# Leaving out TensorE waits that another wait of the same chunk already implies, in a retention layer with a mixture of experts

## The chip, the cores and the metric

The kernel runs on one core of one Trainium2 chip. The metric is the device time of one execution in microseconds (us), the median of several runs. Before the change it is 790.35 us (three runs, 789.27 to 793.92).

## The reference, cut to what matters

The input x has 4 sequences of 1024 tokens with 256 features, all fp32. It is normalised, and two branches read the result: a retention block (attention with a fixed decay instead of a softmax) and a mixture of eight experts with two chosen for each token. The output is x plus both branches.

```
xn = layernorm(x)
# retention: 16 heads of 16
q, k, v = xn @ W_q.T, xn @ W_k.T, xn @ W_v.T
attn = (q @ k.T) * gamma[h] ** (i - j) for j <= i, else 0, divided by sqrt(16)
y = attn @ v, normalised by sequence and head, times gn_weight, plus gn_bias
a = y @ W_o.T
# experts
probs = softmax(xn @ gate_w.T + gate_b); the two largest are kept
f = sum over the two of prob * (relu(xn @ w1[e] + b1[e]) @ w2[e] + b2[e])
out = x + a + f
```

## The kernel before, in words

The kernel is written engine by engine: each engine has its own program, in an order written out by hand, and all coupling goes through semaphores. An engine's `wait_ge(s, n)` holds back all that stands behind it in that engine's program. There is no planner.

The work has four stages. First comes the layer norm and the routing of the tokens to experts. Then comes retention, in 32 chunks of 128 tokens: chunks 0 to 3 and 28 to 31 are written out, chunks 4 to 27 are a loop whose body holds two chunks (`run_steps(pe, 0, NT, 4, 28, chunk)`, line 855). Then come 39 slots of 256 token rows through the experts' two layers (lines 744 and 648), and last the output projection (line 908).

Retention keeps, for each pair of heads, a running state, so that a chunk needs only its own scores and the state. TensorE's order in chunk i is: query projection of chunk i+1 (line 717), key transposes of i+1 (754), the part of the output that comes from the state (`across`, 784), transposes of the tokens of i+2 (695), query transposes of i+1 (760), the new state's sums (807), the part of the output from inside the chunk (`inside`, 796), the scores of i+1 (`scores`, 773), key and value projection of i+2 (704). The results in PSUM are taken out by ScalarE (ACT) and VectorE (DVE): ACT copies the transposed queries into a masked layout in two instructions (`diagonal_queries`, line 539), which the scores of the same chunk need; DVE masks the scores (1084), makes keys and queries from the projections (1072, 1078), and keeps the state (1090, 1096).

GpSimd (POOL) works beside it: for each chunk it issues two indirect DMAs (line 427) that scatter the chunk's normalised rows to their experts' slots. SyncE starts the loads for that scatter when TensorE has signalled the token transposes (`xt_psum`), so the scatter runs at the chunks' pace, about one chunk behind.

The scores are sixteen matmuls in the trace (eight in the source; an fp32 matmul appears as two): four groups of 32 rows of the array, one for each group of four heads, two column blocks each.
Of the kernel before, what the change touches and what calls it, by code (L numbers as in the profile page):

```python
# [36 lines left out]
NT = B * T // P  # L37
# [4 lines left out]
NB = H // HB  # L42
QH = 2
# [68 lines left out]
def wait(eng, sem, value):  # L112

    if isinstance(value, int) and value <= 0:
        return
    eng.wait_ge(sem, value)

def build(nc, where, x, wq_t, wkv_t, wo_t, gn, gate_t, gate_b, w1, w2, b1, b2, const, out):
# [9 lines left out]
    with ExitStack() as ctx:  # L129
# [30 lines left out]
        y_t = xn[:].rearrange("p t (c i) -> p t c i", c=KC)  # L160
# [45 lines left out]
        s_f = ff(NB, HB * P)  # L206
# [4 lines left out]
        q_diag = ff(2, KC, QH * P)  # L211
# [4 lines left out]
        def v_own(par, c=None):  # L216
            pairs = H // QH if c is None else HP // QH
            return bass.AP(v_pad.tensor, v_pad[:, par, (c or 0) * HP * 2 * DH:(c or 0) * HP * 2 * DH + 1].offset,
                           [list(v_pad.ap[0]), [QH * 2 * DH, pairs], [3 * DH, QH], [1, DH]])
# [40 lines left out]
        s = {}  # L260
# [380 lines left out]
        def _(pe):  # L641
# [55 lines left out]

            def key_value_projection(n, par):

                pe.wait_ge(s["xt_h"], n + 1)  # L700
                pe.wait_ge(s["xt_l"], n + 1)
                for m, (a, b) in enumerate(PASSES):
                    for k in range(KC):
                        last = pe.matmul(ps[:, 4, :], xt[:, par, a, k * P:(k + 1) * P], wkv[:, b, k, :],  # L704
                                         start=(m == 0 and k == 0), stop=(m == 2 and k == KC - 1))
                last.then_inc(s["kv_psum"], 1)

            def query_projection(n, par):

                pe.wait_ge(s["xt_h"], n + 1)  # L710
                pe.wait_ge(s["xt_l"], n + 1)

                wait(pe, s["q_t"], n)
                wait(pe, s["q_diag"], QH * n)
                for m, (a, b) in enumerate(PASSES):
                    for k in range(KC):
                        last = pe.matmul(ps[:, 5, 0:D], xt[:, par, a, k * P:(k + 1) * P], wq[:, b, k, :],  # L717
                                         start=(m == 0 and k == 0), stop=(m == 2 and k == KC - 1))
                last.then_inc(s["q_psum"], 1)
# [28 lines left out]

            def key_transposes(n, par):
                pe.wait_ge(s["k_f"], n + 1)  # L750

                wait(pe, s["st_t"], n - 1)
                for c in range(KC):
                    last = pe.transpose(ps[:, 6, c * P:(c + 1) * P], kq_f[:, par, c * P:(c + 1) * P], ident)  # L754
                last.then_inc(s["kt_psum"], 1)
# [6 lines left out]

            def scores(n, par):

                pe.wait_ge(s["k_t"], n + 1)
                pe.wait_ge(s["q_diag"], QH * (n + 1))
                for c in range(KC):
                    for g in range(NB):
                        rows = slice(g * QR, (g + 1) * QR)
                        if c == 0:  # L770

                            wait(pe, s["s_f"], NB * (n - 1) + g + 1 if not isinstance(n, int) or n > 0 else 0)
                        last = pe.matmul(ps[:, g, c * QH * P:(c + 1) * QH * P], kq_t[rows, par, 0, c * P:(c + 1) * P],  # L773
                                         q_diag[rows, par, c], start=True, stop=True)
                        if c == KC - 1:
                            last.then_inc(s["s_psum"], 1)

            def across(n, par):
                pe.wait_ge(s["st_f"], n + 1)
                pe.wait_ge(s["q_t"], n + 1)  # L780

                wait(pe, s["y_t"], n)
                for c in range(KC):
                    last = pe.matmul(ps[:, 7, c * P:(c + 1) * P], state_f[:, c], kq_t[:, par, 1, c * P:(c + 1) * P],  # L784
                                     start=(c == 0), stop=False, skip_group_check=True)
                last.then_inc(s["across_done"], 1)

            def inside(n, par):
                pe.wait_ge(s["s_f"], NB * (n + 1))
                pe.wait_ge(s["v"], n + 1)  # L790

                for c in range(KC):
                    for o in range(QH):
                        for g in range(NB):
                            h = c * HP + g * QH + o
                            last = pe.matmul(ps[g * QR:(g + 1) * QR, 7, c * P:(c + 1) * P], v_pad[:, par, h * 2 * DH:(h + 1) * 2 * DH],  # L796
                                             s_f[:, g, (c * QH + o) * P:(c * QH + o + 1) * P], start=False,
                                             stop=(c == KC - 1 and o == QH - 1), skip_group_check=True)
                last.then_inc(s["y_psum"], 1)

            def state_sums(n, par):
                pe.wait_ge(s["k_f"], n + 1)
                pe.wait_ge(s["v"], n + 1)

                pe.wait_ge(s["k_t"], min(n + 2, NT) if isinstance(n, int) else n + 2)
                for c in range(KC):
                    last = pe.matmul(ps[:, 6, 256 + c * P:256 + (c + 1) * P], kq_f[:, par, c * P:(c + 1) * P], v_own(par, c),  # L807
                                     start=(c == 0), stop=(c == KC - 1), skip_group_check=True)
                last.then_inc(s["u_psum"], 1)

            def chunk(i, par):
                if within(i + 1, NT):
                    query_projection(i + 1, 1 - par)
                if within(i + 1, NT):
                    key_transposes(i + 1, 1 - par)
                if within(i, NT):
                    across(i, par)
                if within(i + 2, NT):
                    x_transposes(i + 2, par)
                if within(i + 1, NT):  # L820
                    query_transposes(i + 1, 1 - par)
                if within(i, NT - 1):
                    state_sums(i, par)
                if isinstance(i, int) and i == NT - 1:
                    layer1(0, 0, (0, 1))
                if within(i, NT):
                    inside(i, par)
                if within(i + 1, NT):
                    scores(i + 1, 1 - par)
                if isinstance(i, int) and i == NT - 2:  # L830
                    pe.wait_ge(s["v"], NT)
                    slot_transposes(0, 0)
                if within(i + 2, NT):
                    key_value_projection(i + 2, par)
# [4 lines left out]
            pe.wait_ge(s["w_split_h"], 3)  # L839
            pe.wait_ge(s["w_split_l"], 3)  # L840
            key_value_projection(0, 0)
            query_projection(0, 0)

            pe.wait_ge(s["route_mask"], 1)
            pe.wait_ge(s["tables_done"], 3)
            for k in range(2):
                last = pe.matmul(ps[:, 1 + k, 0:NT * E], token_sets[:, k], mask_bf[:], start=True, stop=True)
            last.then_inc(s["route_psum"], 1)
            key_transposes(0, 0)
            x_transposes(1, 1)  # L850
            query_transposes(0, 0)
            pe.wait_ge(s["rows_done"], 2)
            scores(0, 0)
            key_value_projection(1, 1)
            run_steps(pe, 0, NT, 4, 28, chunk)

# [442 lines left out]
```

## Time and profile before

| | |
|---|---|
| median of 3 runs | 790.35 us |
| profiled execution, its own time | 788.52 us |
| its span, first to last instruction | 786.7 us |
| mean granted TensorE clock | 0.974 |
| TensorE matmul busy | 732.9 us (93%) |
| VectorE busy | 584.2 us (74%) |
| ScalarE busy | 498.2 us (63%) |
| GpSimd busy | 283.1 us (36%) |

The median is over other executions than the profiled one, which took 788.52 us. A busy time counts the engine's own instructions; waits, register instructions and DMA issues are not in it. The end of a matmul in the trace is modelled, so a signal that a matmul gives is best read from the instruction that waited for it. In the timeline, neighbouring instructions of one line are merged into one row.

### The profile page before, as it was taken

How to read it: one execution, taken by the hardware profiler on the slowest of the kernel's cores; microseconds unless marked ns; L12 is line 12 of the kernel's file. 1: busy time of each engine (PE TensorE's matmuls, PEld its weight loads, DVE VectorE, ACT ScalarE, POOL GpSimd, SP SyncE). 2: the span in 40 equal slices, each digit the busy share in tenths (PEclk: the TensorE clock that was granted, in tenths of full speed). 3: DMA queues.
4: the chain of work that ended last, by engine and by line, in shares of the span. 5: the costliest groups of instructions: out<-in, count | busy, mean ns of one | idle time of the engine just before them, and what ended most of it. 6: DMA issues, size and time to landing. Idle time of an engine off the chain costs nothing.

```text
span 786.7 us, 20206 instructions
## 1 busy us (share of the span) xinstructions
PE 732.9 (93%) x6588; PEld 678.4 (86%) x6588; DVE 584.2 (74%) x1024; ACT 498.2 (63%) x880; POOL 283.1 (36%) x225
## 2 busy tenths in 40 slices
PE   2948999999999988999999999999999999999967
PEld 1426788888887788999999999999999999999957
DVE  6776777777777776877877878777778778778545
ACT  3832334333333386787787787887877877877780
POOL 0013333333334313344344354353353453443420
PEclk9977999999999998999999999999999999999988
DMA  9995333333334485788888888788888888886249
GB/s 294 371 335 176 119 105 108 98 103 101 101 101 136 157 299 150 227 218 252 213 232 251 206 236 257 184 250 242 208 247 239 213 249 227 217 252 173 35 109 332
DMA packets 89047, 157.85 MB, mean 201 GB/s; under 512 B 26496, under 2 KB 66560, under 8 KB 78976
## 3 DMA queue, kind: packets, MB, share of 16 engines
q1 hardware_dynamic: 74720, 138.87, 53.8%
q0 software_dynamic: 14304, 18.69, 14.5%
q8 instruction: 13, 0.21, 0.1%
q14 instruction: 10, 0.08, 0.0%
HBM read 111.67 MB, written 37.37 MB: 189 GB/s over the span
## 4 chain that ended last, share of the span: by engine, by line
PE 85%; DVE 5%; issue 4%; ACT 2%; DMA 2%; POOL 0%; SPq 0%; POOLq 0%; ACTq 0%; DVEq 0%; another core or an unknown queue 0%
PE ps L744 28%; PE ps L648 27%; PE ps L704 6%; PE ps L773 6%; PE ps L717 3%; PE ps L796 3%; PE ps L760 2%; PE ps L908 2%; PE ps L729 2%; PE ps L784 2%; PE ps L666 1%; PE ps L754 1%; PE ps L807 1%; ACT arena_f L539 1%; DMA xn<-x 1%
## 5 line engine op out<-in xcount | busy, mean ns | idle before, releaser
L648 PE MATMUL ps<-arena_r 128*128 128x256 f32 x1872 | 235.2, 286 | 2.2 <-DVE arena_r L1184 2.2
L744 PE MATMUL ps<-arena_r 128*128 128x256 f32 x1872 | 233.4, 285 | 1.9 <-DVE arena_r L1101 1.1
L744 PEld LDWEIGHTS ps<-arena_r 128*128 128x128 f32 x1872 | 229.5, 194 | 2.4 <-issue 2.4
L648 PEld LDWEIGHTS ps<-arena_r 128*128 128x128 f32 x1872 | 228.3, 193 | 2.4 <-issue 2.4
L444 POOL TENSOR_TENSOR fence_out<-eps_col 128x1 f32<-128x1 f32 x39 | 78.7, 2019 | 274.6 <-DVE arena_f L1160 274.6
L498 ACT ACTIVATE arena_r<-arena_f 128x2048 fp32r<-128x2048 f32 x77 | 143.7, 1921 | 0.0
L446 POOL DMA_INDIRECT sum_rows<-arena_f,pair_slot x78 | 122.7, 1574 | 18.1 <-issue 17.3
L580 ACT ACTIVATE arena_f<-ps,arena_f 128x256 f32<-128x256 f32 x156 | 65.3, 471 | 90.5 <-PE ps L744 79.5
L1176 DVE TENSOR_TENSOR arena_r<-arena_f,arena_r 128x2048 fp32r<-128x2048 f32 x39 | 89.4, 2292 | 38.7 <-ACT arena_r L498 38.7
L1184 DVE TENSOR_TENSOR arena_r<-arena_f,arena_r 128x512 fp32r<-128x512 f32 x78 | 55.9, 717 | 53.7 <-ACT arena_r L588 51.9
L1084 DVE TENSOR_TENSOR arena_f<-ps,cst 128x512 f32<-128x512 f32 x128 | 84.7, 683 | 14.9 <-PE ps L773 14.9
L1172 DVE TENSOR_TENSOR arena_r<-arena_f,arena_r 128x2048 fp32r<-128x2048 f32 x38 | 86.8, 2285 | 1.0 <-ACT arena_r L498 1.0
L520 ACT ACTIVATE arena_f<-ps 128x256 f32<-128x256 f32 x32 | 12.3, 384 | 95.0 <-DVE arena_f L1072 81.8
L427 POOL DMA_INDIRECT xs_rows<-pair_chunk,row_chunk x64 | 62.4, 976 | 20.7 <-issue 20.3
L580 ACT ACTIVATE pair_chunk<-ps,arena_f 128x256 f32<-128x256 f32 x156 | 65.5, 472 | 3.3
L1184 DVE TENSOR_TENSOR arena_r<-pair_chunk,arena_r 128x512 fp32r<-128x512 f32 x78 | 50.4, 688 | 12.8 <-ACT arena_r L588 12.8
L773 PE MATMUL ps<-arena_f 32*128 32x256 f32 x512 | 46.2, 409 | 14.4 <-DVE rows L1050 9.2
L704 PE MATMUL ps<-wkv,arena_r 128*128 128x512 f32 x192 | 54.4, 419 | 1.0 <-DVE arena_r L1065 1.0
L773 PEld LDWEIGHTS ps<-arena_f 32*128 32x128 f32 x512 | 30.8, 188 | 24.1 <-issue 13.7
L425 POOL TENSOR_TENSOR fence_out<-eps_col 128x1 f32<-128x1 f32 x32 | 6.1, 190 | 123.5 <-DMA row_chunk<-rows 123.0
L704 PEld LDWEIGHTS ps<-wkv,arena_r 128*128 128x128 f32 x192 | 34.3, 192 | 17.6 <-issue 11.8
L588 ACT ACTIVATE arena_r<-arena_f 128x512 fp32r<-128x512 f32 x78 | 49.3, 632 | 0.0
(134 smaller groups left out, 855.2 us busy)
## 6 DMA issues: line engine op xcount, KB each, us to landing
arena_f<-w SPq DMA_DIRECT2D x78, 1024.0 KB
xs_rows<-spare_rows SPq DMA_DIRECT2D x39, 258.0 KB, 3.6
arena_f<-xs_rows SPq DMA_DIRECT2D x39, 258.0 KB, 3.8
pair_chunk<-xn SPq DMA_DIRECT2D x32, 256.0 KB, 2.6
arena_f<-b SPq DMA_DIRECT2D x39, 128.0 KB, 4.0
xn<-x SPq DMA_DIRECT2D x8, 512.0 KB, 8.8
x_chunk<-xn SPq DMA_DIRECT2D x32, 128.0 KB
arena_f<-sum_rows SPq DMA_DIRECT2D x8, 512.0 KB, 7.6
```

Source lines behind the costliest of these rows:

```text
L444: nc.gpsimd.tensor_tensor(fence_out[:, 0:1], eps_col[:], eps_col[:], ALU.add).then_inc(s["fence"], 1)
L446: nc.gpsimd.indirect_dma_start(sum_rows, bass.IndirectOffsetOnAxis(ap=pair_slot[:, par, j:j + 1], axis=0), ys[:, j * D:(j + 1) * D], None, ...
L498: nc.scalar.activation(parts_[par][:, 0], raw[par], ACT.Copy).then_inc(s[f"w{k + 1}_h"], 1)
L580: last = nc.scalar.activation(h_f[hp][:, o * SLOT:(o + 1) * SLOT], ps[:, H_BANK[hp], o * SLOT:(o + 1) * SLOT], ACT.Relu, bias=b1_slot[:, p ...
L648: last = pe.matmul(out_ap, lhs(a), rhs(b), start=start and n == 0, stop=stop and n == 2, **kw)
L704: last = pe.matmul(ps[:, 4, :], xt[:, par, a, k * P:(k + 1) * P], wkv[:, b, k, :], start=(m == 0 and k == 0), stop=(m == 2 and k == KC - 1))
L744: last = pe.matmul(ps[:, H_BANK[hp], o * SLOT:(o + 1) * SLOT], w1_r[par][:, a, at:at + P], xs_r[:, b, k * SLOT:(k + 1) * SLOT], start=(m = ...
L773: last = pe.matmul(ps[:, g, c * QH * P:(c + 1) * QH * P], kq_t[rows, par, 0, c * P:(c + 1) * P], q_diag[rows, par, c], start=True, stop=True)
L1084: V.tensor_tensor(s_f[:, g].rearrange("p (h i) -> p h i", h=HB), ps[:, g, :].rearrange("p (h i) -> p h i", h=HB), C["causal"].unsqueeze(1) ...
L1172: V.tensor_tensor(w1_r[par][:, 1], w1_raw[par], w1_r[par][:, 0].bitcast(F32), ALU.subtract).then_inc(s["w1_l"], 1)
L1176: V.tensor_tensor(w2_r[par][:, 1], w2_raw[par], w2_r[par][:, 0].bitcast(F32), ALU.subtract).then_inc(s["w2_l"], 1)
L1184: V.tensor_tensor(h_r[:, 1, cols], h_f[hp], h_r[:, 0, cols].bitcast(F32), ALU.subtract).then_inc(s["h_l"], 1)
```

## The change: what it does

From seven functions of TensorE's program it takes wait calls away, fourteen for each chunk of the loop by the diff: the wait for the high half of the tokens in both projections (the low half is computed from the high one) and for the low half in the query projection (the key and value projection of the same chunk stood before it and waited for it); the wait for the masked queries in the query projection; that for the state sum in the key transposes; those for the keys and, four times, for the masked scores in `scores`; that for the copied output in `across`; that for the values in `inside`; and those for keys and values in `state_sums`. Two remain under a condition on the written-out chunk number: the keys' in the first scores, and the values' in the last state sums. No matmul, copy, load or their order is changed. The functions from the diff:

```diff
--- before.py
+++ after.py
@@ -697,7 +697,6 @@
 
             def key_value_projection(n, par):
 
-                pe.wait_ge(s["xt_h"], n + 1)
                 pe.wait_ge(s["xt_l"], n + 1)
                 for m, (a, b) in enumerate(PASSES):
                     for k in range(KC):
@@ -707,11 +706,7 @@
 
             def query_projection(n, par):
 
-                pe.wait_ge(s["xt_h"], n + 1)
-                pe.wait_ge(s["xt_l"], n + 1)
-
                 wait(pe, s["q_t"], n)
-                wait(pe, s["q_diag"], QH * n)
                 for m, (a, b) in enumerate(PASSES):
                     for k in range(KC):
                         last = pe.matmul(ps[:, 5, 0:D], xt[:, par, a, k * P:(k + 1) * P], wq[:, b, k, :],
@@ -748,8 +743,6 @@
 
             def key_transposes(n, par):
                 pe.wait_ge(s["k_f"], n + 1)
-
-                wait(pe, s["st_t"], n - 1)
                 for c in range(KC):
                     last = pe.transpose(ps[:, 6, c * P:(c + 1) * P], kq_f[:, par, c * P:(c + 1) * P], ident)
                 last.then_inc(s["kt_psum"], 1)
@@ -762,14 +755,12 @@
 
             def scores(n, par):
 
-                pe.wait_ge(s["k_t"], n + 1)
+                if isinstance(n, int) and n == 0:
+                    pe.wait_ge(s["k_t"], 1)
                 pe.wait_ge(s["q_diag"], QH * (n + 1))
                 for c in range(KC):
                     for g in range(NB):
                         rows = slice(g * QR, (g + 1) * QR)
-                        if c == 0:
-
-                            wait(pe, s["s_f"], NB * (n - 1) + g + 1 if not isinstance(n, int) or n > 0 else 0)
                         last = pe.matmul(ps[:, g, c * QH * P:(c + 1) * QH * P], kq_t[rows, par, 0, c * P:(c + 1) * P],
                                          q_diag[rows, par, c], start=True, stop=True)
                         if c == KC - 1:
@@ -778,8 +769,6 @@
             def across(n, par):
                 pe.wait_ge(s["st_f"], n + 1)
                 pe.wait_ge(s["q_t"], n + 1)
-
-                wait(pe, s["y_t"], n)
                 for c in range(KC):
                     last = pe.matmul(ps[:, 7, c * P:(c + 1) * P], state_f[:, c], kq_t[:, par, 1, c * P:(c + 1) * P],
                                      start=(c == 0), stop=False, skip_group_check=True)
@@ -787,8 +776,6 @@
 
             def inside(n, par):
                 pe.wait_ge(s["s_f"], NB * (n + 1))
-                pe.wait_ge(s["v"], n + 1)
-
                 for c in range(KC):
                     for o in range(QH):
                         for g in range(NB):
@@ -799,8 +786,8 @@
                 last.then_inc(s["y_psum"], 1)
 
             def state_sums(n, par):
-                pe.wait_ge(s["k_f"], n + 1)
-                pe.wait_ge(s["v"], n + 1)
+                if isinstance(n, int) and n >= NT - 2:
+                    pe.wait_ge(s["v"], n + 1)
 
                 pe.wait_ge(s["k_t"], min(n + 2, NT) if isinstance(n, int) else n + 2)
                 for c in range(KC):
```

## Rows read from the trace of the kernel before

**Rows 1.** The page: busy time by engine; chain that ended last, by line.

```profile
PE 732.9 (93%) x6588; PEld 678.4 (86%) x6588; DVE 584.2 (74%) x1024; ACT 498.2 (63%) x880; POOL 283.1 (36%) x225
...
PE ps L744 28%; PE ps L648 27%; PE ps L704 6%; PE ps L773 6%; PE ps L717 3%; PE ps L796 3%; PE ps L760 2%; PE ps L908 2%; PE ps L729 2%; PE ps L784 2%; PE ps L666 1%; PE ps L754 1%; PE ps L807 1%; ACT arena_f L539 1%; DMA xn<-x 1%
```

**Rows 2.** Timeline (start us, us, engine, line, count, idle before): ends of chunks 3, 27.

```profile
92.65 0.72 PE L704 MATMUL ps<-wkv,arena_r 128*128 128x512 f32 x2
...
248.22 1.66 PE L704 MATMUL ps<-wkv,arena_r 128*128 128x512 f32 x6
```

**Rows 3.** Timeline of one chunk, 151.02 to 157.69: TensorE, POOL, ACT.

```profile
151.02 1.65 PE L704 MATMUL ps<-wkv,arena_r 128*128 128x512 f32 x6
...
153.79 0.96 POOL L427 DMA_INDIRECT xs_rows<-pair_chunk,row_chunk  x1 [0.30 <-issue]
...
154.13 0.43 PE L760 MATMUL ps<-cst,arena_f 128*128 128x128 f32 x2
...
155.32 0.84 ACT L539 ACTIVATE arena_f<-ps,cst 128x256 f32<-128x256 f32 x2 [1.19 <-PE ps L760]
...
156.29 1.47 PE L773 MATMUL ps<-arena_f 32*128 32x256 f32 x16 [0.28 <-ACT arena_f L539]
157.69 0.50 PE L704 MATMUL ps<-wkv,arena_r 128*128 128x512 f32 x1
```

**Rows 4.** Timeline of another chunk, 118.70 to 124.71: the same engines.

```profile
118.70 0.50 PE L704 MATMUL ps<-wkv,arena_r 128*128 128x512 f32 x1
...
121.31 0.96 POOL L427 DMA_INDIRECT xs_rows<-pair_chunk,row_chunk  x1 [0.30 <-issue]
...
121.82 0.42 PE L760 MATMUL ps<-cst,arena_f 128*128 128x128 f32 x2
...
122.28 0.84 ACT L539 ACTIVATE arena_f<-ps,cst 128x256 f32<-128x256 f32 x2 [0.46 <-PE ps L760]
...
123.63 1.15 PE L773 MATMUL ps<-arena_f 32*128 32x256 f32 x16
124.71 1.66 PE L704 MATMUL ps<-wkv,arena_r 128*128 128x512 f32 x6
```

**Rows 5.** Timeline of the chunk behind that one, to 131.16.

```profile
128.04 0.96 POOL L427 DMA_INDIRECT xs_rows<-pair_chunk,row_chunk  x1 [0.30 <-issue]
...
128.62 1.47 PE L796 MATMUL ps<-arena_f 128*32 128x128 f32 x32
130.02 1.22 PE L773 MATMUL ps<-arena_f 32*128 32x256 f32 x16
131.16 1.66 PE L704 MATMUL ps<-wkv,arena_r 128*128 128x512 f32 x6
```

**Rows 6.** Who waited for whom, 87 to 250 us: total us, times, longest.

```profile
PE ps L773 <- ACT arena_f L539: 3.6, 14, 0.4
```

**Rows 7.** Windows, line 773 on TensorE: stretch, length, busy (matmuls in it).

```profile
123.60:123.70 0.10, 0.07 (x4) 1.00 0.81 256
149.60:149.70 0.10, 0.07 (x1) 1.00 0.00 0
...
149.60:149.90 0.30, 0.27 (x3) 1.00 0.53 184
```

**Rows 8.** Sequencer instructions of the wait helper, 149.4 to 150.02: ns min/median/max.

```profile
L116 PEldq ALU_OP  x3: 32/32/36, 149.6 to 149.9; - x3
L116 PEldq FUSED_REGOPS  x1: 37/37/37, 149.5 to 149.5; - x1
```

**Rows 9.** Timeline: keys made by DVE, and the key transposes' weight load.

```profile
152.71 0.42 DVE L1072 TENSOR_TENSOR arena_f<-ps,cst 128x256 f32<-128x256 f32 x1 [0.64 <-PE ps L704]
...
153.19 0.20 PEld L754 LDWEIGHTS ps<-cst,arena_f 128*128 128x128 f32 x2
```

**Rows 10.** Timeline of TensorE in chunk 28, the first behind the loop.

```profile
256.50 0.72 PE L773 MATMUL ps<-arena_f 32*128 32x256 f32 x4 [0.72 <-issue]
257.15 1.66 PE L704 MATMUL ps<-wkv,arena_r 128*128 128x512 f32 x6
```

## The prediction, made before the change was run

> **What bounds the kernel now.** I read the page first: TensorE is busy 93% of the span, and the chain that ended last runs over TensorE's lines, the two expert layers (744, 648) ahead of all [rows 1]. The experts' stage holds none of the edited functions, so 790 us is not the number to look at; retention is. The timeline gives its pace: the 24 chunks of the loop take from 92.65 to 248.22 us, 155.57 us or 6.48 each [rows 2], measured from the first matmul of line 704 to the next chunk's.
>
> Chunks are not alike, so next I laid chunks side by side. One takes 157.69 - 151.02 = 6.67 us [rows 3], another 124.71 - 118.70 = 6.01 [rows 4]. The shorter one has TensorE without a gap: its scores (773) start behind the chunk's own matmuls, and nothing is waited for. In the longer one the scores stand 0.28 us idle until ACT's masked copies (539) are there, and those were late because the signal of the query transposes (760) was: in [rows 3] the transposes' modelled end is 154.13 + 0.43 = 154.56, but the copies start at 155.32; in [rows 4] it is 122.24 and 122.28. What keeps the signal back isn't in a row of its own. It goes with POOL's second scatter issue: that one ends at 154.75 in the long chunk, 3.73 us after line 704 began, and the copies start 0.57 us behind that end; in the short chunk it ends at 122.27, 3.57 us after, just as the signal is given. I call such chunks late and on time. The view of waits counts 14 times that the scores stood for ACT [rows 6], so 14 of the 24 chunks are late. A third kind stands in [rows 5]: the issue ends 129.00 - 124.71 = 4.29 us into the chunk, the copies are on time, but line 796 takes 1.47 us, and the chunk 6.45.
>
> So TensorE's own order bounds the on-time chunks, and in late ones the chain 760, 539, 773. A wait that has long been met matters only where TensorE's sequencer is itself the last to arrive.
>
> **The change, part by part.** *The four waits for masked scores, ahead of the four row groups.* In an on-time chunk all four groups start within 0.10 us [rows 7]: the sequencer had prepared them while TensorE was busy. In a late chunk it is held at the wait for the masked queries, and then makes a register value ahead of each group [rows 8], three of 32 to 36 ns with the dispatch around them: one group starts in the first 0.10 us, and after 0.30 us there are three [rows 7], so the fourth is more than 0.2 us later than it could be. Each group works through its own four matmuls, and line 704, which needs the whole array, begins when the last group is through: 157.69 - 156.29 = 1.40 us after the first score in the late chunk, 124.71 - 123.63 = 1.08 in the on-time one. Without the four waits the late chunk should go like the on-time one: 0.32 us less. In on-time chunks nothing: there the register instructions run beside line 796's matmuls, and if that cover went they would cost the same 0.32 us.
>
> *The keys' wait in the scores.* It goes too, and so one wait is left there, which the first weight load can carry itself. Now the last copy ends at 155.32 + 0.84 = 156.16 and the scores start at 156.29, 0.13 later, with a register instruction between [rows 8]. Where a weight load carries the wait that ends last, the distance is 0.06: the keys end at 152.71 + 0.42 = 153.13, the load starts at 153.19 [rows 9]. That gives 0.07 us a late chunk; between 0 and 0.13 I take the row of the like case.
>
> *The waits in the projections, key transposes, across, inside and state sums.* Each is a semaphore instruction or a rider on a register instruction. In both kinds of chunk lines 704 and 760 show no idle stretch ahead of them [rows 3, 4], so the cover is the matmuls queued ahead. I take 0. Below, nothing is excluded by much: were 50 ns of one exposed in each of 24 chunks, it would be 1.2 us of gain. No row shows it exposed. No wait is added, so there is no loss to bound from new waits; nothing moves past a queue of SyncE or POOL.
>
> The direct sum is 14 x (0.32 + 0.07) = 5.5 us.
>
> *What is late next.* A shorter chunk shifts POOL's issue later within the next one, for that issue follows the chunk before at a nearly fixed distance: 3.73 us into a chunk in [rows 3], 4.29 us behind a 6.01 chunk [rows 5]. A late chunk of 6.67 - 0.39 = 6.28 would bring the next issue to about 3.73 + 0.39 = 4.12. There a chunk lies between the late kind (6.28 by then) and the third kind (6.45, whose gain is at most the 1.14 us of its 773 against 1.08: 0.06). So chunks should settle near 6.25 to 6.35, and 24 x (6.48 - 6.25) = 5.5, 24 x (6.48 - 6.35) = 3.1. The direct sum lies at the upper side; an on-time chunk of 6.01 now and then brings it back. I take 5.3. The bounds are 0 (all given back) and all chunks on time, 24 x (6.48 - 6.01) = 11.3.
>
> Against the profiled execution's own 788.52 us the sum gives 783.2. That execution is 1.8 us under the median of 790.35, inside the runs' spread, so I put the gain to the median: **785.0 us**.
>
> *A rule against the change.* In an on-time chunk four groups start in 0.10 us although four waits stand ahead of them; in a late one only one does [rows 7]. The Trainium skill, page "TensorE: Matmul & The Clock Gate", section "Part 2: What happens when you issue a matmul", says that the sequencer pops the next instruction as soon as it has committed one, so that the next matmul is already queued when the array is done. By that rule met waits cost nothing, and the sum would be 0; by the rows it is 5.3. The on-time chunk agrees with the rule, the late one does not, for there the sequencer had been stopped.
>
> **The rivals.** *Nothing changes* (chance 0.17). By one way (0.05) the spread of the groups isn't the waits' but the row groups' own, when their weights couldn't be loaded ahead; against it stand the register instructions, one between each two groups [rows 8]. By the other (0.12) the held signal follows POOL's issue, so a faster TensorE meets it later in the chunk, and what 773 saves, ACT's copies lose. For it: the copies start 0.57 us behind the issue's end, whatever TensorE does before. Against it: the 0.32 us come after the copies, not before, and a third-kind chunk is 6.45, not 6.67. By both the time is 790.4. The first is what the Trainium skill's rule above would give.
>
> *All chunks on time* (chance 0.20): the shift takes the issue out of the stretch in which it holds the signal. For it: 3.57 us is harmless, 3.73 is not, so small shifts decide. Against: at 4.29 us the hold falls on line 796 and still costs 0.44 us. Gain 11.3, time 779.0.
>
> *Slower, by the supply of instructions* (chance 0.08): in the first chunk behind the loop TensorE stands for "issue" between score matmuls, 0.72 us at once, and that chunk takes 257.15 - 248.22 = 8.93 us against 6.01 [rows 10], so such a stall costs 2.9. Every wait that was an instruction of its own and now is gone moves the code behind it, so stalls may fall on other matmuls in the eight written-out chunks. Two more would eat the gain (790.4 - 5.3 + 5.8 = 790.9), three give 793.8; from two on it decides. For it: retention shows a stall of this size once. Against: nothing is added, and a stall that falls on 704's longer matmuls may as well vanish.
>
> **How the numbers follow.** The forecast, a gain of 3 to 8 us, has 0.55. The range takes in both ends of the unknown shift, from 779.0 (all on time) to 790.5 (nothing): 779.0 to 790.5. A measurement of this kernel tells about 1% from no change, which is 782.4 below and 798.3 above. Faster by over 1%: the all-on-time rival and the edge of the forecast, 0.20 + 0.04 = 0.24. Slower by over 1% needs five or more stalls: 0.04. Within 1%: 0.72.
>
> **What the changed profile would show.** Right: the four groups of 773 start within 0.10 us in late chunks too, 1.08 us from 773 to 704 everywhere, scores 0.06 us behind ACT's second copy, 24 chunks in 149 to 152 us, the experts' stage as before. The step on the four waits is wrong if groups still start 0.11 us apart; the step on the start if the 0.13 stays; the step on the shift if chunks average over 6.4 or under 6.15; the step on covered waits if on-time chunks fall below 6.01. The forecast as a whole is wrong if a new idle stretch stands ahead of another line, or if chunks 0 to 3 or 28 to 31 change by more than 2 us.

## The result, and the profile after

The kernel after takes 788.32 us (median of 19 runs, 783.34 to 790.19), the kernel before 792.56 in the 19 runs that stood beside it (789.27 to 797.34). The ratio is 0.9933, interval 0.9917 to 0.9949. That is a gain of 0.67%, 5.3 us of 792.56 (4.0 to 6.6); the two medians themselves lie 4.24 us apart. The forecast was a gain of 5.3. That the two figures meet to a tenth is luck, for the interval alone is 2.6 us wide. The absolute time of 785.0 was built on a median of 790.35 for the kernel before, which came out at 792.56 over more runs; the measured one lies inside the range of 779.0 to 790.5.

First the page after: the experts' lines (739, 648) have their old 28% and 27% of the chain, and the scores (now line 764) have 5% instead of the 6% of [rows 1].

```profile
PE 733.2 (93%) x6588; PEld 674.5 (86%) x6588; DVE 583.1 (74%) x1024; ACT 498.9 (63%) x880; POOL 284.1 (36%) x225
...
PE ps L739 28%; PE ps L648 27%; PE ps L703 6%; PE ps L764 5%; PE ps L783 4%; PE ps L712 3%; PE ps L895 2%; PE ps L724 2%; PE ps L773 2%; PE ps L666 2%; PE ps L753 2%; PE ps L794 1%; DMA xn<-x 1%; PE ps L747 1%; PE ps L695 1%
```

Then the pace of retention: the timeline of TensorE after, from the first matmul of the key and value projection (now 703) in the loop's first chunk to that of chunk 28, and one before the written-out first chunks.

```profile
65.02 2.29 PE L703 MATMUL ps<-wkv,arena_r 128*128 128x512 f32 x6
...
95.43 1.66 PE L703 MATMUL ps<-wkv,arena_r 128*128 128x512 f32 x6
...
246.11 0.50 PE L703 MATMUL ps<-wkv,arena_r 128*128 128x512 f32 x1
```

The 24 loop chunks take 246.11 - 95.43 = 150.68 us, 6.28 each, against 155.57 [rows 2]: 4.89 less. The two profiled executions differ by only 788.52 - 788.0 = 0.5 us. That of the kernel before is a quick one (788.52 is below all 19 of its runs), and that of the kernel after lost 4.4 us outside the loop. The stretch ahead of 65.02 is 1.39 us longer, as this row of the kernel before shows, the written-out first chunks take 95.43 - 65.02 = 30.41 against 92.65 - 63.63 = 29.02, and what stands behind the loop takes 1.6 us more (of the spans of 786.2 and 786.7). The first of these isn't laid to the change: the same stretch ends anywhere from 63.4 to 65.2 us in the profiles below, with the waits or without.

```profile
63.63 2.93 PE L704 MATMUL ps<-wkv,arena_r 128*128 128x512 f32 x6
```

Now a late chunk after, beside [rows 3]: timeline of TensorE, POOL and ACT.

```profile
208.72 1.65 PE L703 MATMUL ps<-wkv,arena_r 128*128 128x512 f32 x6
...
211.46 0.96 POOL L427 DMA_INDIRECT xs_rows<-pair_chunk,row_chunk  x1 [0.30 <-issue]
...
211.83 0.43 PE L753 MATMUL ps<-cst,arena_f 128*128 128x128 f32 x2
...
212.99 0.84 ACT L539 ACTIVATE arena_f<-ps,cst 128x256 f32<-128x256 f32 x2 [1.16 <-PE ps L753]
...
213.88 1.15 PE L764 MATMUL ps<-arena_f 32*128 32x256 f32 x16 [0.17 <-ACT arena_f L539]
214.96 0.50 PE L703 MATMUL ps<-wkv,arena_r 128*128 128x512 f32 x1
```

The chunk is still late: the query transposes end by the model at 212.26, ACT starts at 212.99, just as before. But the scores follow the second copy's end (213.83) by 0.05 us, not 0.13, and line 703 follows the scores by 1.08, not 1.40. The chunk takes 6.24 us instead of 6.67. All four row groups are under way at once: the windows of line 764 (stretch, length, busy, matmuls) show four in the first 0.10 us, where [rows 7] show one.

```profile
213.85:213.95 0.10, 0.07 (x4) 1.00 0.57 174
```

The instructions of TensorE's sequencer in the wait helper, over the 24 loop chunks, show what is gone; first before, then after (kind, count, ns of one as min/median/max).

```profile
L116 PEldq ALU_OP  x106: 32/32/36, 97.9 to 247.1; - x106
L116 PEldq EVENT_SEMAPHORE  x98: 51/51/51, 92.7 to 248.1; - x98
L116 PEldq FUSED_REGOPS  x12: 37/37/37, 97.8 to 240.5; - x12
```

```profile
L116 PEldq EVENT_SEMAPHORE  x24: 51/51/51, 98.0 to 242.7; - x24
```

216 sequencer instructions became 24, one a chunk. The register instructions between the row groups are gone, and so is most of TensorE's waiting for ACT ahead of the scores: 14 times and 3.6 us before [rows 6], after the times in this row. Two more chunks are late by the start of ACT's copies, but their scores stand for only 0.07 and 0.12 us, which the view does not count; so six chunks of the loop are late, not 14.

```profile
PE ps L764 <- ACT arena_f L539: 0.7, 4, 0.2
```

### The profile page after: what moved, and what is told of

It is laid out like the page before. It is cut to its first block, busy times and chain, and to the rows that moved or that the text cites. A ratio compares the mean times of both kernels' runs of the same rounds, so it can differ in the third digit from the quotient of the medians.

```text
span 786.2 us, 19916 instructions
## 1 busy us (share of the span) xinstructions
PE 733.2 (93%) x6588; PEld 674.5 (86%) x6588; DVE 583.1 (74%) x1024; ACT 498.9 (63%) x880; POOL 284.1 (36%) x225
## 4 chain that ended last, share of the span: by engine, by line
PE 86%; DVE 5%; issue 3%; DMA 2%; ACT 2%; SPq 1%; POOL 0%; POOLq 0%; DVEq 0%; ACTq 0%
PE ps L739 28%; PE ps L648 27%; PE ps L703 6%; PE ps L764 5%; PE ps L783 4%; PE ps L712 3%; PE ps L895 2%; PE ps L724 2%; PE ps L773 2%; PE ps L666 2%; PE ps L753 2%; PE ps L794 1%; DMA xn<-x 1%; PE ps L747 1%; PE ps L695 1%
## 5 line engine op out<-in xcount | busy, mean ns | idle before, releaser
L764 PE MATMUL ps<-arena_f 32*128 32x256 f32 x512 | 44.1, 411 | 12.1 <-DVE rows L1037 9.1
L764 PEld LDWEIGHTS ps<-arena_f 32*128 32x128 f32 x512 | 25.9, 188 | 23.5 <-issue 10.7
```

## The experiments

"Late", "on time" and "third kind" are used as in the prediction. "Hold" means that a signal of TensorE, or its next matmul, comes later than its modelled matmuls explain.

**Which waits.** Two kernels divide the change. The first is the kernel before without the keys' wait and the four masked scores' waits in `scores`; its other nine remain.

```diff
 def scores(n, par):
-    pe.wait_ge(s["k_t"], n + 1)
+    if isinstance(n, int) and n == 0:
+        pe.wait_ge(s["k_t"], 1)
     pe.wait_ge(s["q_diag"], QH * (n + 1))
...
-            if c == 0:
-                wait(pe, s["s_f"], NB * (n - 1) + g + 1 ...)
```

> The kernel before, with the five waits in front of the scores (the keys' and the four for masked scores) left out and all others kept. My theory: the gain comes from these five, in chunks whose masked queries come late. It expects 1.08 us from the first score to line 704 in every loop chunk, 24 loop chunks in 149 to 153 us (before 155.6), and a ratio to the kernel before of 0.992 to 0.996, the same as the whole change (0.9933). The rival that all the waits cost a little each expects about a third of the gain, 0.998. The rival that only the place of the code moved expects a ratio anywhere within 0.995 to 1.005, with the 1.4 us from scores to line 704 still there in late chunks.

The second is the opposite: the kernel after with those five put back, so that only the nine others are gone.

```diff
 def scores(n, par):
-    if isinstance(n, int) and n == 0:
-        pe.wait_ge(s["k_t"], 1)
+    pe.wait_ge(s["k_t"], n + 1)
...
+            if c == 0:
+                wait(pe, s["s_f"], NB * (n - 1) + g + 1 ...)
```

> The whole change, but with the five waits in front of the scores put back; the other nine are left out. My theory expects no gain: ratio 0.999 to 1.001, 24 loop chunks in 154.5 to 156.5 us, late chunks again with 1.39 us from the first score to the next projection. The rival that all the waits cost a little expects two thirds of the gain, 0.995 to 0.996.

Measured: five waits alone 785.81 us, ratio 0.9924 (0.9900 to 0.9948), as much as the whole change; the nine others alone 790.6 us, 0.9983 (0.9962 to 1.0004), no gain that can be told. The loops take 150.80 and 155.35 us. A late chunk of each, ACT and TensorE; without the five waits:

```profile
137.23 0.84 ACT L539 ACTIVATE arena_f<-ps,cst 128x256 f32<-128x256 f32 x2 [1.15 <-PE ps L760]
...
138.12 1.15 PE L771 MATMUL ps<-arena_f 32*128 32x256 f32 x16 [0.16 <-ACT arena_f L539]
139.20 0.50 PE L704 MATMUL ps<-wkv,arena_r 128*128 128x512 f32 x1
```

with them, the nine others gone:

```profile
154.70 0.84 ACT L539 ACTIVATE arena_f<-ps,cst 128x256 f32<-128x256 f32 x2 [1.19 <-PE ps L753]
...
155.67 1.46 PE L766 MATMUL ps<-arena_f 32*128 32x256 f32 x16 [0.28 <-ACT arena_f L539]
157.06 0.50 PE L703 MATMUL ps<-wkv,arena_r 128*128 128x512 f32 x1
```

From the second copy's end to the scores it is 138.12 - 138.07 = 0.05 against 155.67 - 155.54 = 0.13, from the scores to the next projection 1.08 against 1.39. Both sizes come with the five waits and go with them. Without the five, two early chunks still take 1.67 and 1.87 us from the scores to the next projection; I had expected 1.08 in all. In both the second scatter issue ends later in the chunk, 5.40 and 4.99 us in.

**Does the gain need late chunks?** Two kernels in which POOL issues only the first of the two scatters of a chunk; the rows of each token's second expert are not scattered, so 32 of 64 such DMAs are left out. The same edit on the kernel before and on the kernel after:

```diff
-    wait(sp, s[f"scat{par}"], (i - par) * 16 + 32)
+    wait(sp, s[f"scat{par}"], (i - par) * 8 + 16)
...
-    for k in range(2):
+    for k in range(1):
         nc.gpsimd.indirect_dma_start(xs_rows, ...)
```

> The kernel before, with one indirect DMA for each chunk in place of two: the row of each token's second expert isn't scattered (that part of the computation is left out), all waits of TensorE as before. My theory: the signal of the query transposes is held by the second of the two issues, so with one alone no chunk is late, the loop's chunks take 6.0 to 6.1 us and 24 of them 144 to 147 us although all fourteen waits are there. The rival that the waits cost time in every chunk expects 6.3 or more.

> The changed kernel with one indirect DMA for each chunk, the same part of the computation left out as in the run beside it. My theory expects the same time as that run within 0.3%: where no chunk is late, the fourteen waits cost nothing. The rival that the waits cost time in themselves expects it about 5 us faster than that run.

Measured: 775.13 us, ratio 0.9758 (0.9722 to 0.9793), with all waits, and 775.2, 0.9768 (0.9730 to 0.9806), without the fourteen. The waits cost nothing here. The ends of the loop with all waits and the scores of one of its chunks, timeline of TensorE:

```profile
89.97 0.50 PE L704 MATMUL ps<-wkv,arena_r 128*128 128x512 f32 x1
...
148.89 1.15 PE L773 MATMUL ps<-arena_f 32*128 32x256 f32 x16
149.97 0.50 PE L704 MATMUL ps<-wkv,arena_r 128*128 128x512 f32 x1
...
233.97 0.50 PE L704 MATMUL ps<-wkv,arena_r 128*128 128x512 f32 x1
```

and without the fourteen:

```profile
90.51 0.50 PE L703 MATMUL ps<-wkv,arena_r 128*128 128x512 f32 x1
...
234.56 0.50 PE L703 MATMUL ps<-wkv,arena_r 128*128 128x512 f32 x1
```

24 chunks in 144.00 and 144.05 us, 6.00 each, and the scores of line 773 take 1.08 with all their waits in place. So the four waits cost nothing in undisturbed chunks, and 0.32 us where the sequencer has been stopped first; and it is the second scatter issue, or the two in a row, that goes with the hold.

**Is a place in the chunk harmless?** In the kernel after, POOL's addition ahead of the issues is done three times, then four, then five, so that the pair of issues comes later within the chunk.

```diff
-    wait(pool, s["fence"], n)
-    pool.wait_ge(s[f"rc{par}"], ...)
-    nc.gpsimd.tensor_tensor(fence_out[:, 0:1], ...)
+    for k in range(3):                      # then 4, then 5
+        wait(pool, s["fence"], 3 * n + k)
+        if k == 0:
+            pool.wait_ge(s[f"rc{par}"], ...)
+        nc.gpsimd.tensor_tensor(fence_out[:, 0:1], ...)
...
```

> The changed kernel, with two more tiny GpSimd additions ahead of each chunk's scatter, so that the second scatter issue ends some 0.5 to 0.7 us later in each chunk. My theory: what makes chunks late or stretches line 783 is where that issue's end falls: at 3.6 to 3.75 us behind the first matmul of line 703 the query transposes' signal is held, at 4.1 to 4.3 the matmuls of the inside part are; at 4.6 and more nothing was seen. It expects most loop chunks at 6.0 to 6.1 us, 24 of them in 145 to 148 us, ratio 0.986 to 0.990. The rival that the issue's end and the late signal only go together by chance expects no change against the changed kernel, 0.993, with late chunks as before.

> The changed kernel with three extra small GpSimd additions ahead of each chunk's scatter. With two, the second issue ended 4.36 to 4.43 us into the chunk, no query transposes were late, and the inside part (line 784) was stretched in every chunk (6.24 to 6.41 us). My theory: one more moves the issue's end past 4.6 us, where neither is held, and as chunks then take 6.0 us, it moves on to about 4.9 and stays. It expects 24 loop chunks in 144.5 to 147 us and a ratio of 0.984 to 0.989. The rival (any place of the issue holds something) expects 6.25 us or more, 0.994.

> The same with four extra additions: the issue's end at about 5.1 us into a 6.0 us chunk. My theory expects the same as with three, 24 chunks in 144.5 to 147.5 us; if the hold then falls on the last signal of the inside part, due about 5.0 us into the chunk, masked scores start later, and chunks take 6.2 to 6.5. The rival expects 6.25 us or more in either case.

Measured: 788.29 us, ratio 0.9958 (0.9939 to 0.9978); 787.31, 0.9930 (0.9904 to 0.9957); 791.94, 0.9979 (0.9954 to 1.0005). None is better than the kernel after, and my expectation of undisturbed chunks failed. One chunk, timeline of TensorE and POOL, with two additions more:

```profile
154.47 1.66 PE L704 MATMUL ps<-wkv,arena_r 128*128 128x512 f32 x6
...
157.92 0.96 POOL L428 DMA_INDIRECT xs_rows<-pair_chunk,row_chunk  x1 [0.30 <-issue]
...
158.39 1.48 PE L784 MATMUL ps<-arena_f 128*32 128x128 f32 x32
159.80 1.15 PE L765 MATMUL ps<-arena_f 32*128 32x256 f32 x16
160.88 0.50 PE L704 MATMUL ps<-wkv,arena_r 128*128 128x512 f32 x1
```

With four more:

```profile
185.25 1.67 PE L704 MATMUL ps<-wkv,arena_r 128*128 128x512 f32 x6
...
189.11 0.96 POOL L428 DMA_INDIRECT xs_rows<-pair_chunk,row_chunk  x1 [0.30 <-issue]
...
190.19 1.93 PE L765 MATMUL ps<-arena_f 32*128 32x256 f32 x16
192.05 0.50 PE L704 MATMUL ps<-wkv,arena_r 128*128 128x512 f32 x1
```

The second issue ends 4.41 and 4.82 us into these chunks; with three more additions it ends 4.53 to 4.72 in, from the fifth loop chunk on. The hold moves with it: from the query transposes' signal (3.73) to the inside part (1.48 us instead of 1.08 at 4.41), to the inside part or the scores with three more, and with four, in about every other chunk, to the scores (1.86 us instead of 1.08 up to the next projection). The theory that a place from 4.6 us on is harmless fell. It also fits the loop chunk of the kernel after from 107.81, in which the scores last over 2 us: there the second issue ends 5.59 us in. A pair that comes earlier in the chunk was not tried; a single chunk of the kernel before (from 210.08), in which the second issue ends 3.28 us in, takes 6.01.

**Does the pair cause it?** In the kernel after, and then in the kernel before, the second scatter is issued only when the first has landed, with one addition of its own ahead of it. Nothing is left out. (In this diff and the next two, "..." at the head stands for the counts of the additions that POOL waits for, which grow with the added ones.)

```diff
...
     for k in range(2):
+        if k == 1:
+            pool.wait_ge(s[f"scat{par}"], (n - par) * 16 + 16)
+            pool.wait_ge(s["fence"], 2 * n + 1)
+            nc.gpsimd.tensor_tensor(fence_out[:, 0:1], ...)
         nc.gpsimd.indirect_dma_start(xs_rows, ...)
```

> The changed kernel, where GpSimd issues a chunk's second scatter only when the first has landed (one more wait and one more small addition between the two). So far: two issues in a row hold something of TensorE's wherever they end (3.6 to 3.75 us: the query transposes' signal; 4.1 to 4.5: the inside part; 4.6 to 5.6: the scores), one issue alone holds nothing. Theory A: the hold comes with a second issue that overlaps the first one's transfer; it expects loop chunks of 6.0 to 6.1 us, 24 in 144 to 147, ratio 0.976 to 0.985. Theory B: any second issue in a chunk holds; the end moves to about 5.5 us, the hold falls on the scores, and it expects 6.3 us or more and a ratio of 0.992 to 1.0.

> The kernel before, all its waits kept, with the same spacing of the two scatter issues. Theory A: no chunk is late, so the fourteen waits cost nothing, and it takes the same time as the changed kernel with the spacing, within 0.3%. Theory B: late chunks stay, and it is 3 to 6 us slower than that.

Measured: **778.34 us, ratio 0.9836 (0.9812 to 0.9859)**, better than both kernels; on the kernel before 778.99, 0.9849 (0.9825 to 0.9873), so that the fourteen waits are worth 0.1%, inside both intervals. POOL and TensorE in the first of them:

```profile
90.91 0.50 PE L707 MATMUL ps<-wkv,arena_r 128*128 128x512 f32 x1
...
154.04 0.99 POOL L431 DMA_INDIRECT xs_rows<-pair_chunk,row_chunk  x1 [0.15 <-issue]
...
156.74 0.19 POOL L430 TENSOR_TENSOR fence_out<-eps_col 128x1 f32<-128x1 f32 x1 [1.71 <-DMA xs_rows<-pair_chunk,row_chunk]
...
157.13 1.15 PE L768 MATMUL ps<-arena_f 32*128 32x256 f32 x16
157.40 1.20 POOL L431 DMA_INDIRECT xs_rows<-pair_chunk,row_chunk  x1 [0.48 <-issue]
158.21 1.66 PE L707 MATMUL ps<-wkv,arena_r 128*128 128x512 f32 x6
...
236.21 0.50 PE L707 MATMUL ps<-wkv,arena_r 128*128 128x512 f32 x1
```

The loop takes 145.30 us, and from its sixth chunk on every one is 6.00 to 6.02, though as many bytes are scattered: the first issue here ends 2.82 us into a chunk that began at 152.21, the second 0.39 us into the next. The loop of the kernel before with the same spacing takes 146.50 us, with one early chunk of 8.15 in it. By themselves these two don't tell spacing from place, for in nearly all undisturbed chunks the second issue now ends outside the stretch of 3.6 to 5 us; the next experiment does.

**Waiting, or only a gap?** In the kernel after, two additions stand between the two issues and nothing waits for a landing.

```diff
...
     for k in range(2):
+        for r in range(2 * k):
+            pool.wait_ge(s["fence"], 3 * n + 1 + r)
+            nc.gpsimd.tensor_tensor(fence_out[:, 0:1], ...)
         nc.gpsimd.indirect_dma_start(xs_rows, ...)
```

> The changed kernel with two small GpSimd additions between a chunk's two scatter issues and no wait for the first to land. If the overlap of the second issue with the first one's transfer holds TensorE, the hold should shrink as the overlap does, but not vanish: the second issue would begin some 0.8 to 1.0 us behind the first one's end, while that transfer is over about 1.1 us behind it. It expects 24 loop chunks in 145 to 150 us and a ratio of 0.983 to 0.992. If the landing alone matters, it expects the changed kernel's 0.993 and 150 to 152 us.

Measured: 781.33 us, ratio 0.9845 (0.9817 to 0.9873). TensorE and POOL in one chunk:

```profile
151.15 1.66 PE L706 MATMUL ps<-wkv,arena_r 128*128 128x512 f32 x6
...
152.97 0.99 POOL L430 DMA_INDIRECT xs_rows<-pair_chunk,row_chunk  x1 [0.15 <-issue]
153.99 0.48 POOL L429 TENSOR_TENSOR fence_out<-eps_col 128x1 f32<-128x1 f32 x2
154.61 0.99 POOL L430 DMA_INDIRECT xs_rows<-pair_chunk,row_chunk  x1
...
156.07 1.15 PE L767 MATMUL ps<-arena_f 32*128 32x256 f32 x16
157.15 0.51 PE L706 MATMUL ps<-wkv,arena_r 128*128 128x512 f32 x1
```

The second issue ends 4.45 us into the chunk, where the kernels with a pair had a hold, and the chunk is 6.00. The second issue begins 154.61 - 153.96 = 0.65 us behind the first one's end, against 0.30 in a pair (I had expected 0.8 to 1.0). So at this place the spacing of the pair decides. The loop of this kernel takes 145.12 us, and two of its first chunks still take 6.43 and 6.45. Whether the 0.35 us of time counts or the additions between was not told apart.

**The same for the other indirect DMAs.** As the first spaced kernel, and the same wait and addition also between the two accumulating DMAs with which POOL adds the experts' results to `sum_rows` (line 446 of the kernel after).

```diff
...
     for j in range(SJ):
+        if j == 1:
+            pool.wait_ge(s["pairs_out"], 32 * sl + 16)
+            pool.wait_ge(s["fence"], 2 * NT + 2 * sl + 1)
+            nc.gpsimd.tensor_tensor(fence_out[:, 0:1], ...)
         nc.gpsimd.indirect_dma_start(sum_rows, ...)
```

> The changed kernel with the spacing of the two scatter issues in retention, and the same spacing for the two indirect DMAs that add each expert slot's rows to the sums (line 446 of the kernel before). If two such issues in a row hold TensorE in the experts' stage too, it expects the 39 slots some per cent shorter and a ratio to the kernel before under 0.980 (0.9836 with the spacing in retention alone). If the experts' stage is bound by TensorE's own matmuls, whose signals have slack there, it expects 0.983 to 0.985.

Measured: 968.93 us, ratio 1.2185 (1.2122 to 1.2248), far slower. First the view of waits from 300 to 900 us (total us, times, longest), then the page's chain by line:

```profile
DVE arena_f L1149 <- DMA sum_rows<-arena_f,pair_slot: 293.6, 34, 9.6
POOL fence_out L453 <- DMA sum_rows<-arena_f,pair_slot: 117.9, 34, 3.7
```

```profile
DMA sum_rows<-arena_f,pair_slot 41%; PE ps L656 5%; PE ps L711 5%; PE ps L772 3%; PE ps L747 3%; PE ps L791 3%; DVE arena_f L1149 2%; POOL fence_out L448 2%; PE ps L720 2%; PE ps L903 2%; DVE arena_f L1155 1%; PE ps L674 1%; PE ps L781 1%; PE ps L802 1%; DMA xs_rows<-pair_chunk,row_chunk 1%
```

POOL waits up to 3.7 us for the first landing, the second DMA starts only then, and VectorE waits 293.6 us in all for `sum_rows`, which has 41% of the chain. In retention the landing (1.71 us of wait) had cover; in the experts' stage it had none. Whether a pair of these issues holds TensorE in the experts' stage, which the run was to answer, stays open.

**Instruction supply in the written-out chunks.** In the kernel after, TensorE's chunks 0 to 29 are all in the loop.

```diff
-            run_steps(pe, 0, NT, 4, 28, chunk)
+            run_steps(pe, 0, NT, 0, 30, chunk)
```

> The changed kernel, with TensorE's loop over chunks 0 to 29 in place of 4 to 27, so that six written-out chunks are gone from TensorE's code; the waits and the order of work stay. In the changed kernel chunks 1, 2, 4, 7 and 28 stand between score matmuls for issue alone (periods 8.95, 8.44, 7.00, 7.11 and 8.55 us against 6.0). If the supply of code is the cause, these shrink: ratio to the kernel before 0.985 to 0.990, retention from 65.0 to 262 us shorter by 3 to 7 us, fewer 16 KB instruction transfers. If they come from something else (loads, register work), the ratio stays at 0.993.

Measured: 784.63 us, ratio 0.9903 (0.9876 to 0.9931), between the two ratios that I had expected, and its interval overlaps that of the kernel after. The first chunks take 30.41 us as before the edit, and chunk 28, now a loop chunk, is no shorter than when it was written out (8.93 in [rows 10], 8.56 in the kernel after). TensorE there:

```profile
245.44 1.66 PE L703 MATMUL ps<-wkv,arena_r 128*128 128x512 f32 x6
...
250.36 1.08 PE L764 MATMUL ps<-arena_f 32*128 32x256 f32 x3
251.68 1.97 PE L764 MATMUL ps<-arena_f 32*128 32x256 f32 x12 [0.24 <-issue]
...
254.32 0.80 PE L703 MATMUL ps<-wkv,arena_r 128*128 128x512 f32 x1
```

254.32 - 245.44 = 8.88 us: the code was in the loop, and the stall stayed. With one scatter issue a chunk the same chunk, written out, takes 6.36 us, and with the two issues spaced, nothing left out, 6.00.

## Why the prediction was right, point by point

- **The four waits.** Right, in size and place: 1.40 to 1.08 us in late chunks, the groups together in 0.10 us. That the wait calls do it, and not the row groups' own loading, is shown by the two kernels that divide the change.
- **The keys' wait.** Right: 0.13 to 0.05, predicted 0.06.
- **The covered waits.** Right: nine waits gone without the five bring nothing that can be told, and on-time chunks stay at 6.00 to 6.02. One term that the prediction put at nothing was small rather than nothing: in seven of the ten loop chunks of the kernel before that were not late, the four waits still spread the scores (1.10 to 1.22 us up to the next projection), 0.5 us in all.
- **The shift.** Right in sum: 6.28 us a chunk, 150.68 for the loop, predicted 149 to 152. In detail it was off. The chunks don't settle between the kinds; late ones (6.15 to 6.29, six of 24) mostly alternate with the third kind (6.37 to 6.42, nine), seven take 6.00 to 6.09, and two early ones 6.32 and 7.11. What a late chunk saves brings the next issue to 4.0 to 4.3 us (predicted 4.12), where in four cases of six the hold falls on the inside part. So the direct sum, 14 late chunks that each save 0.39, is not how the gain came about: eight of them are late no more. It holds all the same because the 18 others average 6.29 us, close to a late one's 6.24, and that is in part luck.
- **Nothing changes, because waits that have been met cost nothing.** True where no chunk is late (144.00 against 144.05 us), false where the sequencer has been stopped. The rule of the Trainium skill weighed in the prediction ("TensorE: Matmul & The Clock Gate", "Part 2: What happens when you issue a matmul") so agrees with chunks in which the sequencer runs ahead (all four groups within 0.10 us), and not with those behind a stop (one group in 0.10 us) [rows 7].
- **The hold follows POOL's issue and eats the saving.** Only in part: the hold does move with the issue, but the 0.32 us come behind the copies and stay saved.
- **All chunks on time.** Not by this change. The state exists, worth about 10 us of the loop (145.30), and is reached by spacing the issues. Nor does the end of the second issue alone decide, as the prediction's 3.57 and 3.73 us suggest: in the kernel before, the chunks from 99.29 and 106.08 have it at 3.85 and 3.86 us, and ACT's copies start 4.43 us in in the one, late, and 3.66 in the other. What decides between them isn't known.
- **Slower by the supply of instructions.** It did not come, and its evidence was misread: chunk 28's stall [rows 10] stays when the chunk's code is in the loop and goes when the second scatter issue does, or when the two are spaced. The row's "issue" only says that the profile shows no wait.
- **The written-out chunks.** The first changed by 1.39 us, within the 2 us allowed, and the last four by about 0.8. With the pair of issues left where it was, the kernels without the five waits take 29.79, 30.41 and 30.41 us in the first chunks, those with them 29.02 and 28.68; each is a single execution, and no run was made to find the cause.

## What to carry to other kernels

Count a wait that has long been met as free only while its engine's sequencer runs ahead of the array. Look for the place where it was stopped, and price the instructions between that stop and the next matmul there. And when an engine's signal comes late with no wait shown, lay good and bad chunks side by side and look at what other engines issue at that moment: here leaving out the waits gave 0.67%, and parting two DMA issues, with all waits in place, 1.51%.

## What the runs showed of the hardware

Two indirect DMAs that GpSimd issued 0.30 us apart went with TensorE's signals and matmuls coming 0.4 to 0.8 us late in most chunks (the inside part 1.48 us instead of 1.08, the copies' start 0.76 us behind the transposes in [rows 3], the scores 1.86 instead of 1.08); 0.65 us apart, with two small additions between, or a landing apart, they didn't, but for a few early chunks (seven of the 72 loop chunks of these three kernels take 6.17 to 8.15 us, all among the first six). The path is open: no row shows where the signal waits. That the first DMA has not landed yet is not enough: with 0.65 us between, the second issue runs from 0.65 to 1.64 us behind the first one's end, and in the kernel with the wait the first landed only 1.71 us behind it.

A wait against a changing register value costs TensorE's sequencer a register instruction of 32 to 37 ns, or a semaphore instruction of 51 ns. Behind a stop, with the dispatch around them, four such waits put 0.32 us on the path.
